# The seam between a graph attention stage and a relational attention stage: work of the second stage placed into the last steps of the first, and three reorderings in the first stage's step

## The chip, the cores and the metric

The kernel runs on one core of one Trainium2 chip. The metric is the device time of one execution in microseconds, lower is better. All tensors are in the chip's memory when it starts, and the output has to be back there when it ends.

## The reference, cut to what matters

There are 16 graphs with 512 nodes of 128 features. Three pieces of work follow one another: a graph layer, a relational attention, and a feed-forward network. All values are float32.

```python
def _gat(h, adj, W, a, out_features):
    Wh = jnp.matmul(h, W)
    e = Wh @ a[:out_features] + jnp.swapaxes(Wh @ a[out_features:], 1, 2)
    scores = jnp.where(adj > 0, jax.nn.leaky_relu(e, negative_slope=0.2), NEG)
    return jnp.matmul(jax.nn.softmax(scores, axis=1), Wh)
# graph layer
h = _gat(_gat(x, adj, W1, a1, F), adj, W2, a2, F)
h = _layernorm(x + h, g_ln1, b_ln1)
x = _layernorm(h + relu(h @ w_ff1 + b_ff1) @ w_ff2 + b_ff2, g_ln2, b_ln2)
# relational attention, 8 heads of 16
scores = jnp.einsum('bhid,bhjd->bhij', q, k) / np.sqrt(dh)
attn = jax.nn.softmax(scores, axis=-1)
for r in range(4):
    out = out + jnp.einsum('bhij,bhjd->bhid', attn * (adj == r)[:, None], v_r)
x = _ln(x + out @ Wo + bo, g1, beta1)
x = _ln(x + gelu(x @ W1 + b1) @ W2 + b2, g2, beta2)
```

The adjacency matrices of this input hold only 0 and 1. The kernel looks at all of them and takes a short path through the attention (path 0) if no other value is there, a general path (path 1) otherwise.

## The kernel before, in words

Each engine (PE is the matrix engine, DVE the vector engine, ACT the scalar engine, POOL the general one, SP the one that issues most DMAs) has its own program, written out by hand. Semaphores tie them together. There is no scheduler: each engine does its instructions in the order in which they are written, and where one waits, all behind it wait.

**The graph layer** (`graph_layer`) is software-pipelined over graphs. In step t, graph t begins (its x and adjacency are turned and multiplied by the weights), graph t-1 is in its first attention round (k = 0), graph t-2 in its second (k = 1) and its first layer norm, and graph t-3 is in the small feed-forward and its second layer norm. There are 19 steps, 0 to 18, for B = 16 graphs: 0 to 3 are written out, 4 to 14 are a loop, 15 to 18 are written out. Steps 16 to 18 only drain: in step 18 only the feed-forward of graph 15 is left.

In a step, DVE does this in order: scores of the second round (`leak` L666 and `mask` L673 for four chunks of rows), the array of absent edges (`no_edge` L774), scores of the first round (same lines), between them the reciprocal of the second round's sums (`invert`, L700), the sum behind the feed-forward (`y_t` L782), the reciprocal and the scaling of the first round's rows (`scale_rows` L707), statistics and shift of the second layer norm (L717, L724, L738), then sum, statistics and finish of the first layer norm (L794, L717, L724, L731). ACT copies, exponentiates (L645) and takes the inverse roots of the layer norms as a logarithm and an exponential (`rstds`, L651 and L658). `hw` (L610) is ACT's copy of the first round's product out of the bank `pair`; from it PE spreads a row (L467, `spread_row`), and the next step's second-round scores start. `centre` is L633 on ACT, and `xs` (L619) the stage's result. POOL scales `hw_n` (L812), which the second round (`round_two`, L493) waits for, and turns the next graph's adjacency into codes (`encode`, four L381). Codes are turned by PE (L443), kept as bytes in `codes`, and held for the attention.

In step 18 the first graph's queries and keys are made in the bank `pair` and split into three bf16 parts, written to a scratch tensor and read back stacked by heads (`FirstQueries`; L241 product, L221, L226, L231, L236 parts). Also there, `see` ORs all graphs' codes together (L747 to L761) so that the attention can choose its path.

**The attention** (`attention`, a new block with a barrier ahead of it) runs in turns of one graph, each of 8 steps s (2 groups of 4 heads by 4 chunks of rows). In a step PE makes four products `peak` (L1003), each of which DVE reduces to its largest value (L1251), for a place 6 steps ahead (`LEAD = 6`); two products `score` per half step (L1018), whose largest values come from those peaks; and the weighted sums (L1042). ACT exponentiates `prob` (L1116); POOL and DVE multiply by the mask (L1387, L1265). Turn -1 does only what must lie ahead of graph 0: 24 peaks, the values, the masks, queries and keys of graph 1. Before it stand the constants on POOL (L1366 to L1372) and the choice of path (L988, L1235, L1238, then a load of the flag and a branch on every engine).

**The feed-forward** (`feed_forward`) follows. It is not touched.

## Time and profile before

| what | value |
| --- | --- |
| median of 3 runs | 1249.26 us (1248.03 to 1250.36) |
| the profiled execution's own time | 1250.93 us |
| its span in the trace | 1249.1 us |
| PE busy | 1092.9 us (87%) |
| DVE busy | 962.1 us (77%) |
| ACT busy | 742.4 us (59%) |
| POOL busy | 614.3 us (49%) |

The time is read against the profiled execution: 1250.93 us, of which 1249.1 us are the span that the trace shows. Busy time counts an engine at work and not one that is waiting, and it is an average over three stages that are limited differently, so the stages are read one by one. A matrix instruction's end is modelled in the trace, so its busy time is no proof of full speed.

### The profile page before, as it was taken

How to read it: one execution, taken by the hardware profiler on the slowest of the kernel's cores; microseconds unless marked ns; L12 is line 12 of the kernel's file. 1: busy time of each engine (PE TensorE's matmuls, PEld its weight loads, DVE VectorE, ACT ScalarE, POOL GpSimd, SP SyncE). 2: the span in 40 equal slices, each digit the busy share in tenths (PEclk: the TensorE clock that was granted, in tenths of full speed). 3: DMA queues.
4: the chain of work that ended last, by engine and by line, in shares of the span. 5: the costliest groups of instructions: out<-in, count | busy, mean ns of one | idle time of the engine just before them, and what ended most of it. 6: DMA issues, size and time to landing. Idle time of an engine off the chain costs nothing. (4 is left out here: it accounts for less than half of the span.)

```text
span 1249.1 us, 21656 instructions
## 1 busy us (share of the span) xinstructions
PE 1092.9 (87%) x6087; PEld 501.8 (40%) x6087; DVE 962.1 (77%) x2313; ACT 742.4 (59%) x1341; POOL 614.3 (49%) x515
## 2 busy tenths in 40 slices
PE   4588888888888549999999999999999999979996
PEld 3465665665664312233332333323333233234443
DVE  2878878878877537788888888888888888618777
ACT  3477677677675323666666666666666666644442
POOL 3311311311300135878887788878888787900000
PEclk9799999999998857999999999999999999979998
DMA  5222112112100242321333213332133320000000
GB/s 168 92 76 77 50 63 88 50 54 97 50 1 1 86 118 70 106 66 50 111 110 97 69 53 109 110 93 70 57 109 110 89 73 8 2 0 34 34 34 34
DMA packets 49413, 86.50 MB, mean 69 GB/s; under 512 B 8787, under 2 KB 35795, under 8 KB 44246
## 3 DMA queue, kind: packets, MB, share of 16 engines
q1 hardware_dynamic: 46454, 85.56, 22.3%
q10 hardware_dynamic: 2912, 0.40, 0.2%
q8 instruction: 20, 0.33, 0.1%
q14 instruction: 27, 0.22, 0.1%
HBM read 52.12 MB, written 29.36 MB: 65 GB/s over the span
## 5 line engine op out<-in xcount | busy, mean ns | idle before, releaser
L1387 POOL TENSOR_TENSOR b_picked<-b_prob,b_mask 128x512 f32<-128x512 f32 x384 | 473.4, 1260 | 129.8 <-ACT b_prob L1116 129.7
L1251 DVE TENSOR_REDUCE b_top<-b_peak 128x1 f32<-128x512 f32 x512 | 343.6, 687 | 87.7 <-PE b_peak L1003 82.6
L1116 ACT ACTIVATE b_prob<-b_score 128x1024 f32<-128x1024 f32 x256 | 262.0, 1023 | 193.3 <-PE b_score L1018 191.5
L812 POOL TENSOR_TENSOR a_hw_n<-a_hw,a_inv 128x512 f32<-128x512 f32 x16 | 19.5, 1219 | 274.2 <-DVE a_inv L700 261.1
L1042 PE MATMUL b_o_ps<-b_picked,b_dval 128*32 128x512 f32 x1024 | 136.4, 604 | 12.7 <-DVE b_picked L1265 10.2
L1042 PE MATMUL b_o_ps<-b_prob,b_val 128*32 128x512 f32 x1024 | 136.3, 604 | 0.3 <-ACT b_o_t L1127 0.3
L1265 DVE TENSOR_TENSOR b_picked<-b_prob,b_mask 128x512 f32<-128x512 f32 x128 | 113.0, 883 | 1.5 <-ACT b_prob L1116 1.4
L1003 PE MATMUL b_peak<-shared 96*128 96x512 bf16 x256 | 103.4, 409 | 3.6 <-DVE b_top L1251 3.5
L645 ACT ACTIVATE a_att<-a_att,a_least 128x512 f32<-128x512 f32 x128 | 91.1, 716 | 17.3 <-DVE a_least L673 16.8
L1003 PE MATMUL b_peak<-b_k_stack,b_q_stack 96*128 96x512 bf16 x256 | 98.3, 384 | 0.0
L673 DVE CUSTOM_DVE_ANT_0 a_att<-a_att,a_no_edge 128x512 f32<-128x512 f32 x128 | 97.2, 778 | 0.0
L381 POOL TENSOR_SCALAR a_code<-a_adj_in 128x512 bf16<-128x512 int32 x64 | 73.3, 1146 | 38.6 <-DMA a_adj_in<-in_adj 23.7
L493 PE MATMUL a_turn<-a_hw_n,a_att 128*128 128x128 f32 x512 | 63.4, 284 | 25.3 <-POOL a_hw_n L812 25.3
L1504 ACT ACTIVATE c_hid<-c_mid,bff 128x512 f32<-128x512 f32 x64 | 44.0, 688 | 62.6 <-PE c_mid L1482 62.6
L1018 PE MATMUL b_score<-shared 98*128 98x512 bf16 x256 | 77.3, 383 | 0.0
L1018 PE MATMUL b_score<-b_q_stack,b_k_stack 98*128 98x512 bf16 x256 | 76.5, 379 | 0.0
L493 PEld LDWEIGHTS a_turn<-a_hw_n,a_att 128*128 128x128 f32 x512 | 60.8, 198 | 37.4 <-issue 37.4
L479 PE MATMUL a_mid<-a_h_t,wff 128*128 128x512 f32 x128 | 65.1, 636 | 11.1 <-ACT a_h_t L569 11.1
L485 PE MATMUL a_out<-a_hid,wff 128*128 128x512 f32 x128 | 59.2, 605 | 17.8 <-ACT a_hid L639 17.8
L1003 PEld LDWEIGHTS b_peak<-shared 96*128 96x128 bf16 x256 | 25.2, 98 | 113.9 <-DVE b_top L1251 98.8
L651 ACT ACTIVATE a_lnv<-a_mv,eps 128x4 f32<-128x4 f32 x32 | 9.5, 298 | 102.1 <-DVE a_mv L724 102.1
L1003 PEld LDWEIGHTS b_peak<-b_k_stack,b_q_stack 96*128 96x128 bf16 x256 | 24.6, 96 | 108.8 <-DVE b_top L1251 93.8
(176 smaller groups left out, 1807.6 us busy)
## 6 DMA issues: line engine op xcount, KB each, us to landing
a_adj_in<-in_adj SPq DMA_DIRECT2D x16, 1024.0 KB, 5.4
scratch<-shared SPq DMA_DIRECT2D x32, 384.0 KB, 2.6
shared<-scratch SPq DMA_DIRECT2D x16, 768.0 KB, 6.8
scratch<-shared SPq DMA_DIRECT2D x32, 256.0 KB, 2.6
b_q_stack<-scratch SPq DMA_DIRECT2D x8, 768.0 KB, 5.5
b_k_stack<-scratch SPq DMA_DIRECT2D x8, 768.0 KB, 8.0
a_x_in<-in_x SPq DMA_DIRECT2D x16, 256.0 KB, 2.7
xs<-in_x SPq DMA_DIRECT2D x16, 256.0 KB, 5.5
```

Source lines behind the costliest of these rows:

```text
L381: eng.tensor_scalar(code[:, c, :].rearrange("p (k q) -> p k q", k=C), adj_in[:, c, :].rearrange("p (q k) -> p k q", k=C), CODE_HI, CODE_LO ...
L479: pe.matmul(mid[f % 2][:, :], w["wff1"][0][:, f * P:(f + 1) * P], h_t[:, :], start=True, stop=True).then_inc(mid_done, 1)
L493: mm = pe.matmul(turn[:, ic * D:(ic + 1) * D], att[1][:, jc, ic * P:(ic + 1) * P], hw_n[:, jc, :], start=(jc == 0), stop=(jc == C - 1))
L645: act.activation(att[k][:, c, :], att[k][:, c, :], ACT.Exp, bias=least[k][:, c:c + 1], scale=-1.0, accum_out=total[k][:, c:c + 1]).then_in ...
L673: dve.tensor_tensor_reduce(att[k][:, c, :], att[k][:, c, :], no_edge[:, c, :], 1.0, HIGHEST, ALU.add, ALU.min, least[k][:, c:c + 1]).then_ ...
L1003: pe.matmul(peak[hh % 2][:, :], q_stack[par][0:K, h, c * P:(c + 1) * P], k_stack[par][0:K, h, :], start=True, stop=True).then_inc(sem("pea ...
L1018: mm = pe.matmul(score[u][:, k, :], k_stack[par][:, h, c * P:(c + 1) * P], q_stack[par][:, h, :], start=True, stop=True)
L1042: mm = pe.matmul(o_ps[32 * hh:32 * hh + 32, :], v[:, c, GH * g + hh, :], src[:, hh, :], start=(c == 0 and rel is None), stop=(c == C - 1 a ...
L1116: act.activation(prob[s % 2][:, 2 * u:2 * u + 2, :], score[u][:, :, :], ACT.Exp, scale=float(DH) ** -0.5).then_inc(sem("exp_ready"), 1)
L1251: dve.tensor_reduce(top[g][:, hh, c:c + 1], peak[hh % 2][:, :], AX.X, ALU.max, negate=True).then_inc(sem("peak_read"), 1)
L1265: dve.tensor_tensor(picked[(NR * s + rel) % 2][:, hh, :], prob[s % 2][:, hh, :], m, ALU.mult).then_inc(sem("picked_dve"), 1)
L1387: pool.tensor_tensor(picked[(NR * s + rel) % 2][:, hh, :], prob[s % 2][:, hh, :], m, ALU.mult).then_inc(sem("picked_pool"), 1)
```

## The change

What it does, piece by piece:

- **Steps 16 to 18 become a tail written by hand** in each engine's program. Into it go the attention's turn -1: queries and keys of graph 0 and graph 1 and their stores to scratch, graph 0's values, its mask, its 24 peaks with the reductions, and the turning, splitting and loading of the first group's largest values. The attention then starts at turn 0. The 24 products go through three PSUM banks in turn (before: two).
- **The OR of the codes** is one instruction of 512 words per step, behind `scale_rows`; only the last three instructions (`judge`) and the choice of the flag stay in the tail.
- **POOL's `encode`** waits for that OR (`codes_seen`) and no longer for the last mask of the first round (`masked[0]`).
- **The copy `hw`** stands ahead of the first layer norm's inverse root on ACT.
- **The reciprocal of the second round's sums** stands ahead of the fourth `leak` and not behind it.
- **The constants**: the two rows of ones under each key stack come by DMA from an array of ones (before: two memsets on POOL, L1366); graph 0's share of the others is set in step 3.

```diff
@@ FirstQueries
+    def peak(self, pe, banks, n):
+        R6, g, s, hh = 6 * self.z.DH, n // 16, n // 4, n % 4
+        h, c = 4 * g + hh, s % 4
+        if n == 0:
+            pe.wait_ge(self.sem("stacked"), 32)
+        if n >= len(banks):
+            pe.wait_ge(self.sem("peak_read"), n - len(banks) + 1)
+        pe.matmul(banks[n % len(banks)], self.q_stack0[0:R6, h, c * P:(c + 1) * P], self.k_stack0[0:R6, h, :],
+                  start=True, stop=True).then_inc(self.sem("peak_ready"), 1)
...
@@ steps
-            for t in range(B - 1, B + 3):
-                step(t, t < B, t - 1 < B, t - 2 < B, True, False)
+            step(B - 1, True, True, True, True, False)
...
@@ tensor
+            def tail():
+
+                spread_row(1, B - 2)
+                turn_h(B - 3)
...
+                first_qk.product(pe, pair[:, 0, :], 0, 0)
+                first_qk.product(pe, pair[:, 1, :], 0, 1)
+                for f in range(FC):
+                    feed_up(B - 3, f)
+                feed_down(B - 3)
...
+                turn_h(B - 1)
+                peaks(3, 5)
+                turn_n(B - 2)
+                for f in range(FC):
+                    feed_up(B - 1, f)
+                    peaks(5 + 2 * f, 7 + 2 * f)
+                feed_down(B - 1, (13, 15, 16, 16, 16))
+                pe.wait_ge(sem_b("values0_kept"), 2)
+                first_qk.turn_top(pe, row[0])
+                peaks(16, 18)
+                turn_y(B - 1)
+                peaks(18, 20)
+                pe.wait_ge(other_made, 1)
+                pe.transpose(pair[0:1, 1, 0:P], other[:, :], ident[:, :]).then_inc(other_turned, 1)
+                turn_n(B - 1)
+                peaks(20, 24)
@@ scalar
                 if feed:
                     rstds(1, t - 3)
                     centre(t - 3)
+                if first:
+                    keep_hw(t - 1)
                 if second:
                     rstds(0, t - 2)
-                if first:
-                    act.wait_ge(hw_done, t)
...
@@ vector
                 for c in chunks:
                     if c + 1 < C:
+                        if c == 2:
+                            between()
                         leak(k, b, c + 1, s2)
-                    if c == 2 and k == 0:
-                        between()
                     mask(k, b, c)
...
+            def see(b):
+                words = codes[:, b, :, :].rearrange("p c n -> p (c n)").bitcast(I32)
+                first = isinstance(b, int) and b == 0
+                if not first:
+                    dve.wait_ge(codes_seen, b)
+                dve.tensor_tensor(seen[:, :], words if first else seen[:, :], words, ALU.bitwise_or).then_inc(codes_seen, 1)
...
                     invert(0, t - 1)
                     scale_rows(t - 1)
+                    see(t - 1)
...
+                most(0, 16)
+                first_qk.split_top(dve, row[0])
+                add_h(B - 1)
+                most(16, 18)
+                norm_stats(1, B - 1)
+                most(18, 20)
+                norm_shift(B - 1)
...
+                most(20, 24)
@@ gpsimd
                 if more:
                     if first:
-                        pool.wait_ge(masked[0], C * t)
+                        pool.wait_ge(codes_seen, t)
                     encode(pool, t + 1, range(C))
...
@@ attention
-            for b in range(-1, 2):
-                turn(b, b % 2)
+            for b in range(2):
+                turn(b, b)
```

On DVE, inside a loop step of the graph layer, from the third `mask` of the first round to the statistics of the second layer norm, before:

```order
L666 SCALAR_TENSOR_TENSOR a_att<-a_row,a_s_own,a_low 128x512
L700 RECIPROCAL a_inv<-a_total 128x4
L671 REGISTER_ALU
L673 ISA a_att,a_least<-a_att,a_no_edge 128x512
```

and at the same place in the change, with what now stands behind the row scaling:

```order
L897 RECIPROCAL a_inv<-a_total 128x4
L863 SCALAR_TENSOR_TENSOR a_att<-a_row,a_s_own,a_low 128x512
L868 REGISTER_ALU
L870 ISA a_att,a_least<-a_att,a_no_edge 128x512
...
L904 TENSOR_SCALAR a_xw_n<-shared,a_inv 128x130
L943 TENSOR_TENSOR a_seen<-a_seen,codes 128x512
L914 BN_STATS a_stats<-a_mid 128x6 x4
```

The reciprocal has changed places with the fourth `leak`, and one instruction `seen` of 128x512 has come in ahead of the statistics.

On ACT, at the end of a loop step, from the centring of graph t-3 (`a_y`) to the result `xs`, before:

```order
L633 ACTIVATE a_y<-a_mid,a_shift,a_rstd 128x128 x4
L651 ACTIVATE a_lnv<-a_mv,eps 128x4
L658 ACTIVATE a_rstd<-a_lnv 128x4
L610 COPY a_hw<-a_pair 128x520
L614 REGISTER_ALU
L615 ISA
```

and in the change:

```order
L829 ACTIVATE a_y<-a_mid,a_shift,a_rstd 128x128 x4
L809 COPY a_hw<-a_pair 128x520
L847 ACTIVATE a_lnv<-a_mv,eps 128x4
L854 ACTIVATE a_rstd<-a_lnv 128x4
L738 REGISTER_ALU
L739 ISA
```

The copy `a_hw` has moved ahead of the logarithm and the exponential.

On PE, the seam of the two stages from the last transposes of the graph layer to the attention's first scores, before (L988 reads the flag, L1054 are queries and keys of graph 1, L1003 peaks, L1018 scores):

```order
L988 MATMUL b_misc<-ident,other 1x128
L942 TENSOR_LOAD b_general
L942 ISA x2
L943 COMPARE_AND_BRANCH
L1054 MATMUL b_misc<-xs,wq 128x512
L1054 MATMUL b_misc<-xs,wk 128x512
L1003 MATMUL b_peak<-shared 128x512 x17
L1069 MATMUL b_misc<-ident,b_top 16x128
L1003 MATMUL b_peak<-shared 128x512 x8
L1018 MATMUL b_score<-shared 128x512 x2
```

and in the change (L305 are the peaks in the tail, L567 and L573 the feed-forward of graph 15, L1245 a peak and L1260 the scores of turn 0):

```order
L305 MATMUL a_pair<-shared 128x512
L567 MATMUL a_mid<-a_h_t,wff_0 128x512
L305 MATMUL a_row<-shared 128x512
L305 MATMUL a_turn<-shared 128x512
...
L1186 TENSOR_LOAD general
L1186 ISA x2
L1187 COMPARE_AND_BRANCH
L1245 MATMUL b_peak<-shared 128x512
L1260 MATMUL b_score<-shared 128x512 x2
```

24 peaks now stand among the feed-forward and the transposes of graph 15, and behind the branch one peak and the first scores follow at once.

## Rows read from the trace of the kernel before

**Rows 1.** Windows (length, busy of PE, PEld, DVE, ACT, POOL, clock, DMA): four stretches.

```profile
326.15:349.65 23.50, 19.38 (x129) 14.31 (x128) 19.42 (x54) 16.71 (x39) 5.80 (x5) 1.00 0.19 67
...
418.75:447.20 28.45, 13.47 (x32) 6.09 (x32) 14.67 (x20) 8.71 (x16) 3.64 (x3) 0.68 0.38 111
447.20:480.19 32.99, 22.80 (x44) 6.61 (x45) 17.64 (x30) 6.04 (x14) 12.18 (x12) 0.50 0.39 114
480.19:1095.00 614.81, 602.38 (x3581) 187.00 (x3579) 511.51 (x919) 398.39 (x611) 503.44 (x412) 1.00 0.27 78
```

**Rows 2.** Timeline of a loop step: start and length in us, engine, instruction, [idle before].

```profile
336.70 0.75 DVE L666 SCALAR_TENSOR_TENSOR a_att<-a_row,a_s_own,a_low 128x512 f32<-128x512 f32 x1
...
337.79 1.22 POOL L812 TENSOR_TENSOR a_hw_n<-a_hw,a_inv 128x512 f32<-128x512 f32 x1 [16.73 <-DVE a_inv L700]
338.03 1.52 DVE L673 CUSTOM_DVE_ANT_0 a_att<-a_att,a_no_edge 128x512 f32<-128x512 f32 x1
...
339.15 3.81 PE L493 MATMUL a_turn<-a_hw_n,a_att 128*128 128x128 f32 x32 [1.10 <-POOL a_hw_n L812]
...
339.88 4.82 POOL L381 TENSOR_SCALAR a_code<-a_adj_in 128x512 bf16<-128x512 int32 x4 [0.87 <-DVE a_least L673]
...
340.77 1.75 DVE L707 TENSOR_SCALAR a_xw_n<-shared,a_inv 128x130 f32 x4 [0.15 <-DVE a_inv L700]
...
343.44 0.89 DVE L717 BATCH_NORM_STATS2 a_stats<-a_mid 128x6 f32<-128x128 f32 x4 [0.91 <-PE a_mid L425]
...
345.46 0.16 DVE L738 SCALAR_TENSOR_TENSOR a_shift<-a_mv,a_rstd 128x4 f32<-128x4 f32 x1 [0.60 <-ACT a_rstd L658]
345.66 1.50 ACT L633 ACTIVATE a_y<-a_mid,a_shift,a_rstd 128x128 f32<-128x128 f32 x4 [0.23 <-DVE a_shift L738]
...
347.89 0.30 ACT L651 ACTIVATE a_lnv<-a_mv,eps 128x4 f32<-128x4 f32 x1 [0.73 <-DVE a_mv L724]
...
348.33 0.57 ACT L610 COPY a_hw<-a_pair 128x520 f32<-128x520 f32 x1
348.57 1.12 DVE L731 TENSOR_SCALAR a_y<-a_y,a_mv,a_rstd 128x128 f32<-128x128 f32 x4 [0.72 <-ACT a_rstd L658]
348.81 0.20 ACT L615 COPY a_s_own<-shared 128x4 f32 x1
...
350.33 1.41 DVE L666 SCALAR_TENSOR_TENSOR a_att<-a_row,a_hw,a_low 128x512 f32<-128x512 f32 x2 [0.65 <-issue]
```

**Rows 3.** Timeline: the row scaling of step 15, in which POOL encodes nothing.

```profile
363.92 0.88 DVE L707 TENSOR_SCALAR a_xw_n<-shared,a_inv 128x130 f32<-128x130 f32 x4
```

**Rows 4.** Tile view: the shift of 128x4 in the attention and in the graph layer.

```profile
L1337 DVE SCALAR_TENSOR_TENSOR b_shift<-b_mv,b_rstd x16: 161/519/1116, 550.1 to 1107.6; 128x4 f32<-128x4 f32 x16
L738 DVE SCALAR_TENSOR_TENSOR a_shift<-a_mv,a_rstd x16: 161/164/165, 85.6 to 443.2; 128x4 f32<-128x4 f32 x16
```

**Rows 5.** Timeline of the seam, from step 18 to the attention's first score.

```profile
425.35 1.02 PE L241 MATMUL a_pair<-xs,wk 128*128 128x512 f32 x2
...
426.29 3.70 PE L485 MATMUL a_out<-a_hid,wff 128*128 128x512 f32 x8
...
427.87 2.28 DVE L747 TENSOR_TENSOR a_att<-codes 128x2048 int32<-128x2048 int32 x1
...
436.93 0.69 DVE L755 TENSOR_TENSOR a_att<-a_att 128x512 int32<-128x512 int32 x1
...
439.18 0.74 DVE L782 SCALAR_TENSOR_TENSOR a_y_t<-a_out,columns,a_h_t 128x512 f32<-128x512 f32 x1
...
446.15 0.78 ACT L619 ACTIVATE xs<-a_mid,columns 128x512 f32<-128x512 f32 x1 [1.21 <-PE a_mid L431]
...
452.58 2.08 PE L1054 MATMUL b_misc<-xs,wq 128*128 128x512 f32 x2 [4.97 <-issue]
...
464.38 9.05 DVE L1251 TENSOR_REDUCE b_top<-b_peak 128x1 f32<-128x512 f32 x13 [1.87 <-PE b_peak L1003]
```

**Rows 6.** Line view of the peaks: min, median, max ns at PE.

```profile
L1003 PE MATMUL b_peak<-shared x256: 377/382/634, 458.1 to 1031.3; 96*128 96x512 bf16 x128
```

More of the change, by code:

```diff
@@ new lines, in move @@
+    def move(self, sp):
+        R6 = 6 * self.z.DH
+        sp.dma_start(self.x_own[:, :], self.xs[:, 0, :, :].rearrange("p c d -> p (c d)")).then_inc(self.sem("x_own"), 16)
+        load_ones(sp, self.w, self.k_stack0).then_inc(self.sem("ones_in0"), 16)
+        for b in range(2):
+            for n in range(2):
+                for t in range(3):
+                    sp.wait_ge(self.sem(f"part{t}_ready{n}"), b + 1)
+                    store_part(sp, self.scratch[b], self.parts[n], n, t).then_inc(self.sem(f"parts_out{n}"), 16)
+            if b == 0:
+                for n in range(2):
+                    sp.wait_ge(self.sem(f"parts_out{n}"), 48)
+                    sp.dma_start((self.q_stack0, self.k_stack0)[n][0:R6, :, :],
+                                 stack_rows(self.scratch[0, n])).then_inc(self.sem("stacked"), 16)
@@ new lines, in values, with keep_values @@
+    def values(self, pe, bank, half):
+        D, w = self.z.D, self.w
+        for k in range(2):
+            c = 2 * half + k
+            at = bank[:, 2 * k * D:2 * (k + 1) * D]
+            pe.matmul(at, w["ones"][:, :], w["bias3"][:, 0:2 * D], start=True, stop=False)
+            mm = pe.matmul(at, self.x_own[:, c * P:(c + 1) * P], w["wv"][:, 0:2, :].rearrange("p r d -> p (r d)"),
+                           start=False, stop=True)
+        mm.then_inc(self.sem("values0_done"), 1)
+    def keep_values(self, act, bank, half):
+        D, DH = self.z.D, self.z.DH
+        act.wait_ge(self.sem("values0_done"), half + 1)
+        for k in range(2):
+            c = 2 * half + k
+            src = bank[:, 2 * k * D:2 * (k + 1) * D].rearrange("p (r h d) -> p r h d", r=2, h=HEADS)
+            act.copy(self.val0[:, c, :, 0:DH], src[:, 0, :, :])
+            last = act.copy(self.dval0[:, c, :, 0:DH], src[:, 1, :, :])
+        last.then_inc(self.sem("values0_kept"), 1)
@@ new lines, in mask @@
+    def mask(self, act, half):
+        chunks = slice(2 * half, 2 * half + 2)
+        act.copy(self.mask0[:, chunks, :], self.codes[:, 0, chunks, :])
+    def peak(self, pe, banks, n):
[7 more added lines that the diff above has]
+                  start=True, stop=True).then_inc(self.sem("peak_ready"), 1)
@@ L258, with load_ones @@
+def load_ones(eng, w, stack):
+    rows = stack[6 * 16:6 * 16 + 2, :, :].rearrange("r h n -> r (h n)")
+    return eng.dma_start(rows.rearrange("r (a q) -> r a q", q=P), w["ones"][0:2, :].unsqueeze(1).to_broadcast([2, HEADS * 4, P]))
 BLOCKS = 6
@@ L909, in count @@
             def count(turn, end):
-                return sum(0 <= t + by < end for t in range(-2, turn + 1)
+                return sum(0 <= t + by < end for t in range(turn + 1)
                            for n, (_, _, _, by) in enumerate(ITEMS[path]) if t < turn or n < pos)
```

421 lines of the change are left out of this document (273 added, 148 removed).

## The prediction

> **What bounds the kernel now.** I read the windows by stage first, then the timeline of one loop step, then the timeline of the seam. The attention runs 614.81 us with PE busy for 602.38 of them at a granted clock of 1.00 [rows 1]: it is PE's, the change leaves its turns 0 to 15 as they are, and they move as a block. The change works on two other places.
>
> The first is the loop step of the graph layer, 23.50 us long, in which neither PE (19.38 busy) nor DVE (19.42) is full [rows 1]. A chain through four engines sets it. DVE's scores end in the reciprocal of the second round; POOL scales `hw_n` at 337.79 (it had idled 16.73 us for that reciprocal); PE's second round starts at 339.15, 1.10 us idle for POOL; behind it PE turns the feed-forward's result, for which DVE's statistics wait 0.91 us until 343.44. They give the shift at 345.46 and ACT's centring until 345.66 + 1.50 = 347.16. Then ACT does logarithm, exponential, the copy `hw` at 348.33, and two more, and only then the lowered row, for which DVE's next `leak` waits until 350.33 [rows 2].
>
> The second is the seam. Step 18 takes 28.45 us and turn -1 another 32.99 [rows 1], 61.44 us together, with every engine half idle. In step 18 the OR of the codes holds DVE from 427.87 to 439.18, and `y_t`, which PE waits for, stands behind it; the stage ends with `xs` at 446.15 + 0.78 = 446.93, PE's first product comes at 452.58, and from 464.38 the reductions of the peaks run back to back, 9.05 / 13 = 0.70 us each [rows 5].
>
> **The change part by part.**
>
> *Copy ahead of the root.* Between the centring's end (347.16) and the logarithm (347.89) ACT has 0.73 us in which it waits for DVE; the copy takes 0.57 and fits. What followed the copy moves up by 348.81 - 348.33 = 0.48 us. DVE can take it: its layer norm ends at 348.57 + 1.12 = 349.69, 0.64 ahead of the `leak` [rows 2]. Gain 0.48 per step.
>
> *Reciprocal ahead of the fourth leak.* It comes earlier by that instruction, 0.75 us (336.70), and with it POOL, PE's second round and the statistics [rows 2]. The mask behind it stalls on POOL's scaling either way (1.52 us at 338.03 [rows 2]), once, so DVE's scores end as before. Gain 0.75, if the statistics find DVE free.
>
> *The OR in the step.* 0.69 us for 128x512 [rows 5], fifteen times on DVE. What hides it is the 0.91 us wait for PE [rows 2], and that shrinks by the 0.75 above. But POOL's encoding (339.88, 4.82 us) now starts behind the OR, and so no longer runs beside the row scaling, which took 1.75 us with it and 0.88 without [rows 2, 3]. So scaling ends at 340.77 + 0.88 = 341.65, the OR at 342.4, and the statistics could start at 343.44 - 0.75 = 342.69. It fits by 0.3 us; without that cover it would cost up to 0.69 a step.
>
> *Encoding later.* It runs from about 342.7 to 347.4. PE needs the codes behind the next step's transposes, from about 349: 1.6 us to spare. What it newly meets is the shift of 128x4, which would now be issued at 345.46 - 0.75 = 344.7, in the midst of the encoding. It reads two arrays in SBUF. In the graph layer before, with POOL idle, it never took over 0.165 us; in the attention, with POOL busy, 0.161 / 0.519 / 1.116 [rows 4]. So it costs between 0 and 0.95 us, and the centring and DVE's whole rest of the step stand behind it. I take the median, 0.519 - 0.161 = 0.36: both engines' rhythm is fixed here, so the true value is one number within the bounds, and I can't place it better.
>
> This is where a rule of the Trainium skill speaks against the change. "SBUF — State Buffer", section "Who interferes with whom", says that a vector instruction with two SBUF inputs contends with a GpSimd instruction that reads SBUF, and that the one that comes second blocks for the whole instruction of the other. By that rule the shift waits for the rest of an encoding instruction, the OR would too if it ran beside one (it doesn't, POOL waits for it), and the statistics, with one input, don't. The trace agrees, with the spread from 0.161 to 1.116.
>
> *Sum of the steps.* 0.48 + 0.75 - 0.36 = 0.87 us in steps 3 to 14 (twelve): 10.4. Step 15 has no encoding, 1.2. Against that the first OR stands ahead of DVE's preparation in step 1 (0.69), and in step 2 the copy ahead of the root waits for a slow first round: I take 1.2 together. **A = -10.4 us**; bounds from 12 x 0.28 - 1 = 2 to 12 x 1.23 + 1 = 16.
>
> *Steps 16 and 17.* They take on, for two graphs, four products of 1.02 us on PE [rows 5], four first and four second parts on ACT, four remainders on DVE like a `leak` (0.75 [rows 2]), four third parts on POOL that meet DVE's masks as above, and three short instructions that judge the OR. In step 16 DVE has no slack: remainders 1.5, one or two collisions 1, and some of ACT's parts ahead of `hidden`. In step 17 DVE had long waits and takes its share there. Against it stand the 0.48 of the copy twice and the 0.75 of the reciprocal. **B = +1 us**, between -1 and +4.
>
> *The seam.* Now 61.44 us. Then, counted on DVE from the end of step 17: 24 reductions x 0.70 = 16.7 [rows 5]; splitting, `y_t`, statistics, shift and flag 3.3. PE holds it up in the middle: a feed-forward product (3.70 / 4 = 0.93 [rows 5]) and two peaks (2 x 0.38 [rows 6]) against 1.40 of DVE, 0.3 to 0.5 four times, and the last product's 3.70 with three peaks, 4.8 against 2.1: 4.3 in all. The last four peaks stand behind the transposes of the centred array: 1.50 for the centring, 0.9 around it. Sum 26.7. Then the barrier, load of the flag and branch: from 446.93 to 452.58 it was 5.65, with the flag's making in it, which is now done earlier; I take 4.8 (4 to 5.65), and 0.7 for a peak and the scores. 32.2 in all. The parts, stacks and rows of ones are on SP's queue some 20 us before the peaks need them, and graph 1's stack, issued behind the branch, has two attention steps. **C = 32.2 - 61.4 = -29.2 us**, between -25 and -32.
>
> **Sum:** -10.4 + 1 - 29.2 = -38.6. The profiled execution took 1250.93, so 1212.3; it stands 1.67 above the median of the runs, 1249.26, so I forecast a median of **1211**.
>
> **The rivals.**
>
> 1. *The collision eats the loop's gain.* Each shift (or the OR, if statistics come sooner than I count) pays the full price: 0.95, leaving 0.28 per step and A at 2 to 3 us. For it: the row scaling paid 1.75 - 0.88 = 0.87 beside POOL [rows 2, 3]. Against: the median. 1219.
> 2. *The tail runs at the lower clock.* In step 18 the granted clock averaged 0.68, in turn -1 it was 0.50, the level of 1.2 GHz [rows 1]. At that level PE's share of the tail (24 peaks 9.1, feed-forward 7.4, transposes 2.5) doubles from 19 to 38 us, against 26.7 counted: +11, 1222. Against: the tail keeps PE busy where before it sat still for the OR.
> 3. *Slower.* The attention enters behind 5 us without PE work and stays at the lower clock. Each microsecond there loses half, PE being busy 602.38 of 614.81 [rows 1]; from 77 us on at that level the change loses, 1251. Against: before, it came out of 33 us at 0.50 and the attention's mean was still 1.00. The Trainium skill ("TensorE: Matmul & The Clock Gate", Part 1) says that the throttled state is the default and that activity releases it, which would speak for an early rise too.
> 4. *The change doesn't do what it says:* the prologue's chain (parts, scratch, stack, largest values) isn't ready when the tail wants it, and engines wait there. Half of C's overlap lost, 1226.
> 5. *Better:* the shift falls into a gap between two encodings and the branch costs 4: 1203.
>
> **How the numbers follow.** My forecast (1205 to 1216) 0.52, rival 1 0.20, rival 2 0.12, rival 3 0.03, rival 4 0.03, rival 5 0.10. From 1203 to 1223 the range takes in the forecast, rivals 1 and 2 and the edge of rival 5. No change means within 0.2%, about 2.5 us, which is what a measurement of this kernel can tell. All cases but rival 3 are faster: 0.96, 0.01, 0.03.
>
> **What would show it.** The distance of two lowered rows in the loop: 22.6 us (23.2 by rival 1). The row scaling at 0.88, the shift between 0.16 and 1.1, the statistics' wait gone to near zero. From the last layer-norm finish of graph 15 to the end of the stage about 27 us, the first `score` near 441, and 610 us of attention behind it. Wrong would be: a clock of 0.50 over the tail, a wait of PE for `stacked`, encodings that end after PE wants them, or an attention longer than 616.

## The result, and the profile after

| | before | after |
| --- | --- | --- |
| median | 1249.02 us (1248.03 to 1250.36, 4 runs) | 1198.62 us (1197.11 to 1200.78, 4 runs) |
| ratio | | 0.9597 (0.958 to 0.9615) |
| span of the profiled execution | 1249.1 us | 1196.6 us |

The changed kernel is 50.4 us faster by the medians (52.5 by the two spans). The forecast was 1211, the range 1203 to 1223: the sign was right, the gain was too small by 12 us, and the range missed the time by 4.4 us.

The windows of the changed kernel, with the columns of [rows 1]: a loop step; the tail's second part from its first lowered row to the last layer-norm finish; from there to the attention's first score; the attention.

```profile
312.73:335.11 22.38, 19.62 (x128) 14.38 (x128) 18.97 (x56) 16.79 (x40) 5.52 (x5) 1.00 0.20 71
379.56:399.06 19.50, 15.75 (x73) 9.11 (x71) 14.16 (x46) 9.99 (x23) 3.27 (x3) 1.00 0.32 100
399.06:428.97 29.91, 18.17 (x57) 8.07 (x57) 17.84 (x40) 11.68 (x27) 1.96 (x5) 0.75 0.05 12
430.06:1041.09 611.03, 600.04 (x3560) 186.14 (x3560) 509.23 (x914) 396.56 (x608) 499.91 (x409) 1.00 0.29 81
```

The stretches of before that answer to the second and third are these:

```profile
396.01:418.69 22.68, 15.11 (x60) 8.54 (x60) 10.58 (x37) 10.11 (x23) 1.04 (x1) 0.85 0.01 1
418.69:480.19 61.50, 36.27 (x76) 12.71 (x77) 32.31 (x51) 14.75 (x30) 15.82 (x14) 0.58 0.39 112
```

So the seam became 61.50 - 29.91 = 31.6 us shorter and the step ahead of it 22.68 - 19.50 = 3.2. The attention moved as a block: from first to last `b_prob` 610.1 us before (481.3 to 1091.4), 611.0 after (430.1 to 1041.1). All before the seam is read off ACT's first lowered row of each step:

| first `a_low` of step | 4 | 6 | 14 | 16 | 17 |
| --- | --- | --- | --- | --- | --- |
| before, us | 89.73 | 137.04 | 326.15 | 372.82 | 396.01 |
| after, us | 88.83 | 133.82 | 312.73 | 356.83 | 379.56 |

By step 16 the change has gained 372.82 - 356.83 = 16.0 us; step 16 itself gives 0.5 more. From step 6 to 14 a step is (326.15 - 137.04) / 8 = 23.64 us before and (312.73 - 133.82) / 8 = 22.36 after: 1.28 each, where the forecast had 0.87.

The timeline of that loop step, to be laid beside [rows 2]:

```profile
312.73 0.59 ACT L822 ACTIVATE a_low<-a_row 128x512 f32<-128x512 f32 x1
...
323.83 1.04 POOL L1064 TENSOR_TENSOR a_hw_n<-a_hw,a_inv 128x512 f32<-128x512 f32 x1 [12.37 <-DVE a_inv L897]
...
328.14 0.69 DVE L943 TENSOR_TENSOR a_seen<-a_seen,codes 128x512 int32<-128x512 int32 x1
...
329.14 4.72 POOL L467 TENSOR_SCALAR a_code<-a_adj_in 128x512 bf16<-128x512 int32 x4 [4.26 <-DVE a_seen L943]
...
329.30 0.89 DVE L914 BATCH_NORM_STATS2 a_stats<-a_mid 128x6 f32<-128x128 f32 x4 [0.48 <-PE a_mid L513]
...
331.32 0.16 DVE L935 SCALAR_TENSOR_TENSOR a_shift<-a_mv,a_rstd 128x4 f32<-128x4 f32 x1 [0.60 <-ACT a_rstd L854]
331.52 1.51 ACT L829 ACTIVATE a_y<-a_mid,a_shift,a_rstd 128x128 f32<-128x128 f32 x4 [0.23 <-DVE a_shift L935]
...
332.91 0.60 ACT L809 COPY a_hw<-a_pair 128x520 f32<-128x520 f32 x1
```

The OR is hidden: behind it the statistics still wait 0.48 us for PE. The shift is issued while POOL encodes (329.14 to 333.86) and yet takes 0.16 us, in all eleven full loop steps. That is the collision term of the sum, and it wasn't paid. The seam, in the order of time:

```profile
397.98 1.08 DVE L928 TENSOR_SCALAR a_y<-a_y,a_mv,a_rstd 128x128 f32<-128x128 f32 x4
...
399.05 0.68 DVE L311 TENSOR_REDUCE top<-a_pair 128x1 f32<-128x512 f32 x1
...
404.01 0.69 DVE L311 TENSOR_REDUCE top<-a_turn 128x1 f32<-128x512 f32 x1 [1.88 <-PE a_turn L305]
404.62 0.68 DVE L311 TENSOR_REDUCE top<-a_pair 128x1 f32<-128x512 f32 x1
...
412.92 0.28 DVE L321 CAST top_hi<-a_row 16x128 bf16<-16x128 f32 x1 [1.14 <-PE a_row L316]
...
418.25 0.14 DVE L1020 TENSOR_SCALAR general<-a_widest 1x1 int32<-1x1 f32 x1
421.20 0.69 DVE L311 TENSOR_REDUCE top<-a_turn 128x1 f32<-128x512 f32 x1 [2.81 <-PE a_turn L305]
...
423.00 0.68 DVE L311 TENSOR_REDUCE top<-a_turn 128x1 f32<-128x512 f32 x1
```

```profile
419.62 1.11 PE L519 MATMUL a_mid<-ident,a_y 128*128 128x128 f32 x4 [4.19 <-ACT a_y L829]
...
428.57 0.61 PE L1245 MATMUL b_peak<-shared 96*128 96x512 bf16 x1 [6.01 <-issue]
428.97 1.06 PE L1260 MATMUL b_score<-shared 98*128 98x512 bf16 x2
```

The stage ends with DVE's last reduction at 423.68, PE's first product comes 4.9 us later, and DVE had sat 2.81 us ahead of the last four reductions, for peaks that stand on PE behind the transposes of the last centred array.

### The profile page after: what moved, and what is told of

It is laid out like the page before. It is cut to its first block and busy times, and to the rows that moved or that the text cites. A ratio compares the mean times of both kernels' runs of the same rounds, so it can differ in the third digit from the quotient of the medians.

```text
span 1196.6 us, 21640 instructions
## 1 busy us (share of the span) xinstructions
PE 1076.5 (90%) x6087; PEld 496.7 (42%) x6087; DVE 948.1 (79%) x2324; ACT 741.5 (62%) x1341; POOL 602.8 (50%) x513
## 5 line engine op out<-in xcount | busy, mean ns | idle before, releaser
L1489 DVE TENSOR_REDUCE top<-b_peak 128x1 f32<-128x512 f32 x488 | 327.8, 687 | 89.4 <-PE b_peak L1245 85.2
L1622 POOL TENSOR_TENSOR b_picked<-b_prob,mask 128x512 f32<-128x512 f32 x192 | 236.2, 1257 | 61.7 <-ACT b_prob L1360 61.6
L1622 POOL TENSOR_TENSOR b_picked<-b_prob,b_mask 128x512 f32<-128x512 f32 x192 | 237.3, 1263 | 53.6 <-ACT b_prob L1360 53.6
L1064 POOL TENSOR_TENSOR a_hw_n<-a_hw,a_inv 128x512 f32<-128x512 f32 x16 | 16.7, 1041 | 211.8 <-DVE a_inv L897 198.9
L1245 PE MATMUL b_peak<-b_k_stack,b_q_stack 96*128 96x512 bf16 x256 | 98.3, 384 | 0.0
L1245 PE MATMUL b_peak<-shared 96*128 96x512 bf16 x232 | 89.9, 389 | 6.0 <-issue 6.0
L1260 PE MATMUL b_score<-shared 98*128 98x512 bf16 x256 | 77.6, 384 | 0.0
L1260 PE MATMUL b_score<-b_q_stack,b_k_stack 98*128 98x512 bf16 x256 | 76.5, 380 | 0.0
L573 PE MATMUL a_out<-a_hid,wff 128*128 128x512 f32 x128 | 59.5, 605 | 18.5 <-ACT a_hid L835 18.5
L1286 PE MATMUL b_o_ps<-b_picked,b_dval 128*32 128x512 f32 x512 | 68.2, 604 | 7.7 <-DVE b_picked L1503 5.2
L1286 PE MATMUL b_o_ps<-b_picked,dval 128*32 128x512 f32 x512 | 68.2, 604 | 5.0 <-DVE b_picked L1503 5.0
L1245 PEld LDWEIGHTS b_peak<-b_k_stack,b_q_stack 96*128 96x128 bf16 x256 | 24.6, 96 | 108.7 <-DVE top L1489 93.8
L1286 PE MATMUL b_o_ps<-b_prob,b_val 128*32 128x512 f32 x512 | 68.2, 604 | 0.3 <-ACT b_o_t L1371 0.3
L1286 PE MATMUL b_o_ps<-b_prob,val 128*32 128x512 f32 x512 | 68.2, 605 | 0.0
L593 PE MATMUL a_pair<-a_xw_n,a_att 128*128 128x130 f32 x512 | 62.4, 281 | 4.8 <-DVE a_xw_n L904 4.8
```

Source lines behind the costliest of these rows:

```text
L593: mm = pe.matmul(pair[:, ic // 2, at:at + D + 2], att[0][:, jc, ic * P:(ic + 1) * P], xw_n[:, jc, :], start=(jc == 0), stop=(jc == C - 1))
L1245: pe.matmul(peak[hh % 2][:, :], q_stack[par][0:K, h, c * P:(c + 1) * P], k_stack[par][0:K, h, :], start=True, stop=True).then_inc(sem("pea ...
L1260: mm = pe.matmul(score[u][:, k, :], k_stack[par][:, h, c * P:(c + 1) * P], q_stack[par][:, h, :], start=True, stop=True)
L1286: mm = pe.matmul(o_ps[32 * hh:32 * hh + 32, :], v[:, c, GH * g + hh, :], src[:, hh, :], start=(c == 0 and rel is None), stop=(c == C - 1 a ...
L1489: dve.tensor_reduce(top[g][:, hh, c:c + 1], peak[hh % 2][:, :], AX.X, ALU.max, negate=True).then_inc(sem("peak_read"), 1)
L1622: pool.tensor_tensor(picked[(NR * s + rel) % 2][:, hh, :], prob[s % 2][:, hh, :], m, ALU.mult).then_inc(sem("picked_pool"), 1)
```

## The experiments

Each lists the median and its ratio to the kernel before with the 95% interval. "Step" is the distance of the first lowered rows from step 6 to step 14, divided by 8. It tells more than the total: executions with the same code in steps 0 to 3 reached step 4 between 86.96 us (the kernel with the old norm order) and 88.83 us (the changed kernel), so two totals can differ by about 2 us before the loop begins. A second spread lies behind the attention, where no run changed anything: from the last `b_prob` to the feed-forward's first product (`c_mid`) it is 16.7 to 16.9 us in nine of the fourteen profiles, at a mean granted clock of 0.91 to 0.95, and 18.2 to 19.0 us in five (the kernel before, the reciprocal alone, the codes alone, the loop's three edits, the step without the OR), at 0.67 to 0.73.

### The three edits of the loop, one by one and together

**Copy alone**, on the kernel before:

```diff
+                if first:
+                    ... act.copy(hw ...).then_inc(hw_ready, 1)
                 if second:
                     rstds(0, t - 2)
-                if first:
-                    ... act.copy(hw ...).then_inc(hw_ready, 1)
```

> The kernel before, with one edit: in each step ACT's copy hw stands ahead of the first layer norm's inverse root. Recorded theory: the copy fits into the 0.73 us in which ACT waits for DVE's statistics, so what follows moves up by 0.48 us; 13 steps with both (3 to 15) and two more in the drain make -6 to -7 us, 1242 to 1243 us, a loop step of 23.16 instead of 23.64 us. Rival: the root now comes later by what is left of the copy, DVE's layer-norm finish with it, and DVE's next leak then waits for nothing else; the gain would be 0 to 0.2 us a step, 1246 to 1249 us.

Measured: 1242.26 us, 0.9947 (0.9931 to 0.9964); step 23.09, -0.55. The theory held, a little better than its 0.48.

**Reciprocal alone**, on the kernel before:

```diff
                     if c + 1 < C:
+                        if c == 2:
+                            between()
                         leak(k, b, c + 1, s2)
-                    if c == 2 and k == 0:
-                        between()
```

> The kernel before, with one edit: the reciprocal of the second round's sums stands ahead of the fourth leak. POOL still encodes behind the last mask, beside the row scaling. Recorded theory: the chain through POOL, PE's second round and DVE's statistics moves up by 0.75 us, in the 12 or 13 full steps: -9 to -10 us, 1239 to 1240 us, a loop step of 22.9 us. Rival 1: the shift, issued 0.75 us earlier, now falls into the last encoding instruction (which ends at 344.70 us in the step read) and pays up to 0.95 us: no gain. Rival 2: the row scaling at 1.75 us beside the encoding ends at 342.5 us and holds the statistics, so 0.5 us a step and not 0.75: 1242 us.

Measured: 1242.2 us, 0.9936 (0.9919 to 0.9952); step 23.41, only -0.23. Rival 2 named the right place; that its total (1242) came true is partly luck, since it had 0.5 us a step, and this execution was 2.3 us ahead by step 4 (87.44 for 89.73). Timeline of the loop step, DVE and POOL:

```profile
311.67 4.72 POOL L381 TENSOR_SCALAR a_code<-a_adj_in 128x512 bf16<-128x512 int32 x4 [1.48 <-DVE a_least L673]
...
312.67 2.64 DVE L707 TENSOR_SCALAR a_xw_n<-shared,a_inv 128x130 f32 x4 [0.15 <-DVE a_inv L700]
...
315.23 0.88 DVE L717 BATCH_NORM_STATS2 a_stats<-a_mid 128x6 f32<-128x128 f32 x4
```

PE has the statistics' input ready sooner, but the row scaling now takes 2.64 us beside the encoding (1.75 in [rows 2], 0.88 with POOL idle [rows 3]), and the statistics follow it without a wait. Most of the 0.75 us stays there. Where POOL encodes nothing the reciprocal gives it all: steps 15 and 16 take 22.30 us each, for 23.17 and 23.19 before.

**OR and encoding alone**, on the kernel before (step 18 keeps only the three instructions that judge the OR):

```diff
                     scale_rows(t - 1)
+                    see(t - 1)
...
-                        pool.wait_ge(masked[0], C * t)
+                        pool.wait_ge(codes_seen, t)
```

> The kernel before, with one edit: the OR of the codes as one instruction of 512 words a step behind the row scaling, POOL's encoding behind it; in step 18 only the three short instructions that judge it. Copy and reciprocal stand where they stood. Step 18 loses 11.3 us of OR on DVE and gets back 2.0: -9.3 us where y_t waited for it, -4 to -9 if PE's chain is next. In the loop, recorded theory: the OR is hidden (scaling ends 0.87 us sooner), the shift collides with the encoding at 0.36 us a step on average, +4 us: 1243 to 1245 us. Rival: the shift meets no instruction in its way and takes 0.16 us, as in the changed kernel: loop step unchanged at 23.64 us, 1240 us.

Measured: 1246.33 us, 0.9971 (0.9961 to 0.9981); step 24.01, **+0.37**. Here the shift does collide, in all ten steps of the window from 100 to 350 us (tile view of that window: least, median, greatest ns):

```profile
L738 DVE SCALAR_TENSOR_TENSOR a_shift<-a_mv,a_rstd x10: 605/619/629, 111.5 to 327.6; 128x4 f32<-128x4 f32 x10
```

In the step read, an encoding instruction begins at 327.05 (the row below covers it and the next, 1.11 us of work each) and so ends near 328.16. The shift, issued at 327.56, ends at 328.18:

```profile
327.05 2.31 POOL L381 TENSOR_SCALAR a_code<-a_adj_in 128x512 bf16<-128x512 int32 x2
```

That the step's +0.37 is so near the 0.36 of the theory is luck: the shift is 0.46 longer, of which some 0.2 is won back behind it (see below), and it is issued 0.11 later behind the lowered row (19.42 us for 19.31).

By step 16 this kernel is 6.35 us behind (379.17 against 372.82), 2.0 of them before step 4 already. From the last layer-norm finish (424.60) to the first score (476.12) it then takes 51.5 us where the kernel before took 61.50: the OR's removal from step 18 is worth 10.0 us.

**All three, with the old steps 16 to 18 and turn -1:**

```diff
+ the three diffs above together
```

> The kernel before with all three edits of the step (copy, reciprocal, OR with encoding behind it), but with steps 16 to 18 and turn -1 as they were. It measures term A with the same steps as the recorded sum, apart from the tail. Recorded theory: 0.87 us a step, A = -10.4 us, and step 18 without the OR: -9.3 us; together 1229 us. By the trace of the changed kernel (22.37 us a step, -16.0 us by step 16): 1223 us. If the three edits hinder or help one another, the sum of the three single ones (taken over the loop step) differs from this one's.

Measured: 1224.07 us, 0.9788 (0.977 to 0.9806); step 22.36, exactly the changed kernel's; at step 16 356.92 us, 15.9 ahead. The expectation from the trace held (1223), the recorded sum didn't (1229). The three single effects add to -0.55 - 0.23 + 0.37 = -0.41 us a step, the three together give -1.28. The 0.87 between them is two collisions that each edit has alone and not in company: the row scaling's with the old place of the encoding, and the shift's with its new place. By the single runs they cost 0.75 - 0.23 = 0.52 and 0.37, 0.89 together.

**The encoding back behind the mask**, on the changed kernel:

```diff
-                        pool.wait_ge(codes_seen, t)
+                        pool.wait_ge(masked[0], C * t)
```

> The changed kernel with one edit: POOL's encoding waits for the last mask of the first round again, as before the change; copy, reciprocal and OR stay. Theory: the encoding then lies beside the row scaling, which takes 2.64 us as in the kernel with the reciprocal alone (0.88 now), and the OR behind it waits too; the statistics come 1.2 to 2 us later than now: a loop step of 23.4 us or more, +12 us: 1208 to 1216 us. So the encoding's move is what lets the reciprocal's 0.75 us through. Rival: copy and reciprocal give their 0.48 + 0.23 us by themselves and the OR is hidden: 22.95 us a step, 1205 us.

Measured: 1210.78 us, 0.9694 (0.9678 to 0.971); step 23.56, +1.20. The theory's time held. Timeline:

```profile
337.35 5.21 POOL L467 TENSOR_SCALAR a_code<-a_adj_in 128x512 bf16<-128x512 int32 x4 [1.48 <-DVE a_least L870]
...
338.34 2.64 DVE L904 TENSOR_SCALAR a_xw_n<-shared,a_inv 128x130 f32 x4 [0.15 <-DVE a_inv L897]
...
340.91 0.68 DVE L943 TENSOR_TENSOR a_seen<-a_seen,codes 128x512 int32<-128x512 int32 x1
341.51 0.88 DVE L914 BATCH_NORM_STATS2 a_stats<-a_mid 128x6 f32<-128x128 f32 x4
```

Copy, reciprocal and OR without the encoding's move are worth 23.64 - 23.56 = 0.08 us a step. The scaling is at 2.64 us again, the OR follows it and the statistics follow the OR, none of them with a wait: the OR is no longer hidden. So the 1.20 that the move is worth are the 0.75 - 0.23 = 0.52 of the reciprocal and the 0.68 of the OR. The copy doesn't need it: alone, with the encoding in its old place, it gave its 0.55.

### Is the shift's 0.16 us luck of the phase?

In the changed kernel an encoding instruction runs from 330.32 to 331.43 and the next begins at 331.51 (tile rows of one instruction each, below). The shift, issued at 331.32, ends at 331.48, in the gap.

```profile
330.32 1.11 POOL L467 TENSOR_SCALAR a_code<-a_adj_in 128x512 bf16<-128x512 int32 x1
331.51 1.14 POOL L467 TENSOR_SCALAR a_code<-a_adj_in 128x512 bf16<-128x512 int32 x1
```

**OR left out of the step, encoding earlier:**

```diff
-                    see(t - 1)
...
-                        pool.wait_ge(codes_seen, t)
+                        pool.wait_ge(scaled[0], t)
```

> The changed kernel with less work: the OR of the codes is left out of every step (the look then sees graph 15's codes only, which changes no path for this input), and POOL's encoding starts behind the row scaling itself, about 0.65 us sooner. Theory of the phase: a shift issued while an encoding instruction runs ends when that instruction ends. Instructions of 1.18 us that began at 329.14 us end at 330.32 and 331.50, so the shift issued at 331.32 pays nothing; beginning at 328.5 they end at 330.86 and 332.04, and the shift pays 0.5 to 0.56 us. So with less work the kernel is slower by 12 x 0.5 = 6 us: 1204 to 1206 us, shift at 0.65 to 0.75 us, a loop step of 22.9 us. Rival: a small operand of 128x4 waits only by chance, the shift stays near 0.16 us and the time at 1198 to 1199 us; or the OR was on the path, and the time falls below 1195 us.

**Encoding later by one small instruction:**

```diff
+            if not isinstance(b, int):
+                eng.tensor_scalar(idle[:, :], adj_in[:, 0, 0:128], CODE_HI, CODE_LO, ALU.min, ALU.max)
             for c in chunks:
```

> The changed kernel with one more instruction of POOL ahead of each encoding in the loop (128 columns into an array that nobody reads, some 0.35 us). Nothing waits for it but the encoding. Theory of the phase: the border between two encoding instructions moves from 331.50 to about 331.85 us, the shift issued at 331.32 waits for it: 0.5 us instead of 0.16, +0.35 us a step in 11 steps, +3.5 to +4 us: 1202 to 1203 us. Rival: the price is a fixed one for any meeting; the shift stays at 0.16 us and the time at 1198 to 1199 us.

The shift in the same window, without the OR and then with the delay:

```profile
L935 DVE SCALAR_TENSOR_TENSOR a_shift<-a_mv,a_rstd x11: 697/729/745, 107.0 to 333.0; 128x4 f32<-128x4 f32 x11
```

```profile
L938 DVE SCALAR_TENSOR_TENSOR a_shift<-a_mv,a_rstd x11: 467/479/507, 106.3 to 331.1; 128x4 f32<-128x4 f32 x11
```

Its length was foretold for both (0.65 to 0.75 us, and 0.5), and is neither a chance nor a fixed price. The times moved less than foretold: without the OR 1200.32 us, 0.9597 (0.9581 to 0.9613), step 22.60, +0.23 and not 0.5; with the delay 1197.87 us, 0.9584 (0.9568 to 0.96), step 22.48, +0.12 and not 0.35. The totals can't be told from the changed kernel's (without the OR the stretch behind the attention was 18.2 us for 16.8, 1.4 of its 1.7 more); the steps can. The reason is what follows the shift. From its end to the statistics of the first norm (with the sum `add_x` between) it is 0.85 us in the changed kernel (331.48 to 332.33), but 0.64 without the OR (333.73 to 334.37), 0.63 with the delay (331.58 to 332.21) and 0.63 in the kernel with the codes' edit alone (328.18 to 328.81): behind a blocked shift the next instruction starts 0.2 us closer. So without the OR the shift is 0.57 longer, 0.22 of it comes back, and the statistics are 0.12 sooner: 0.23. With the delay 0.32 - 0.22 = 0.10. Even so, a step with less work is longer, because the encoding starts 0.72 us sooner in it (15.69 us behind the lowered row for 16.41). A kernel without the OR whose encoding keeps its place was not run.

### The tail

**Old order of the norms in its second part** (ACT's roots and centring follow it):

```diff
                 judge()
+                norm_stats(1, B - 2)
+                norm_shift(B - 2)
                 add_x(B - 1)
                 norm_stats(0, B - 1)
-                norm_stats(1, B - 2)
                 norm_finish(B - 1)
-                norm_shift(B - 2)
```

> The changed kernel with one edit in the tail's second part (graph 15 in its second round): statistics and shift of the second layer norm of graph 14 stand ahead of the sum and the first layer norm of graph 15 again, and ACT's roots and centring in that order, as in step 17 of the kernel before. Theory: this order, not the parts, made steps 16 and 17 shorter where the sum had +1 us: the first layer norm of graph 15 ends 2 us later and all of the seam with it: 1200 to 1201 us. Rival: DVE and PE do the same work in another order, and the reductions of the peaks wait for no norm: 1198 to 1199 us.

Measured: 1200.5 us, 0.9604 (0.9588 to 0.962). From the second part's first lowered row (377.76) to the end of the last norm finish (398.24 + 1.12 = 399.36) it is 21.60 us, against 19.50: the 2.1 us that the theory had. DVE's reciprocal comes 9.07 us behind the lowered row in both, so the difference lies behind it. The window of that stretch, to be laid beside 379.56:399.06:

```profile
377.76:399.36 21.60, 15.91 (x73) 9.05 (x71) 14.51 (x46) 11.48 (x27) 3.27 (x3) 0.97 0.29 90
```

The total moved by 1.9, within what two executions differ by; the stretch is what shows it.

**Two banks for the 24 peaks, not three:**

```diff
-        peak_banks = [pair[:, 0, :], row[1][:, :], turn[:, :]]
+        peak_banks = [pair[:, 0, :], row[1][:, :]]
...
-                peaks(0, 3)
+                peaks(0, 2)
...
-                peaks(3, 5)
+                peaks(2, 5)
```

> The changed kernel with the 24 first peaks going through two PSUM banks in turn, as in turn -1 of the kernel before (three in the changed one). Theory 1: the third bank is why the reductions follow one another at 0.60 to 0.69 us and not at the 0.70 us of the recorded sum; with two they go at 0.70, +1.4 us: 1200 us. Theory 2: the pace is DVE's own and the 0.70 us belonged to the lower clock of turn -1; then 1198 to 1199 us, and the reductions at 0.64 us where PE is at the full clock.

Measured: 1199.0 us, 0.9599 (0.9583 to 0.9615). By the total theory 2 held, and at the full clock most reductions follow one another at 0.60 to 0.69 us with two banks too. The stretch shows a part of theory 1 as well. Where a peak takes PE 0.61 us instead of 0.38, one reduction follows the other after 0.79 (398.62 to 399.41) and 0.78 us (420.72 to 421.50), where three banks have 0.59 and 0.60, and once DVE waits 0.27 us for a peak. From the last norm finish to the end of the last reduction it is 25.35 us (397.44 to 422.79) against 24.6: the third bank is worth 0.7 us, half of what theory 1 had.

**Last four peaks ahead of the last transposes:**

```diff
+                peaks(20, 24)
                 turn_n(B - 1)
-                peaks(20, 24)
```

> The changed kernel with one edit in the tail: the last four peaks stand ahead of the transposes of the last centred array on PE, not behind. In the changed kernel DVE had done everything at 418.39 us and waited 2.81 us for them until 421.20. Theory: the four reductions then run during the centring, and the stage ends with xs at 421.55 us instead of with the last reduction at 423.68: -2.1 us, 1196 to 1197 us. Rival: the peaks run into PE's transposes or the barrier waits for something else (the row of ones on SP's queue, POOL's start of the block at 423.96 us): 1198 to 1199 us.

Measured: 1194.79 us, 0.9563 (0.9547 to 0.9578). The theory held. DVE's last four reductions run from 418.12 on, while ACT centres; from the last norm finish to the first score:

```profile
398.70:426.59 27.89, 18.47 (x56) 8.03 (x57) 17.75 (x40) 11.67 (x27) 1.95 (x5) 0.78 0.05 11
```

That is 27.89 us against 29.91. The total is 3.8 us lower; 2.0 of it are this edit's. In the kernel with both edits below, the same stretch is 28.60 us (397.74 to 426.34), 0.4 of the difference on the way from the last instruction to PE's first product.

**xs behind the lowered row, and both together:**

```diff
                 if second:
                     lower(1, t - 2)
+                if feed and not (isinstance(t, int) and t == 3):
+                    keep_x(t - 4)
...
-                if feed:
-                    keep_x(t - 3)
```

> The changed kernel with one edit in the step: ACT's write of xs stands behind the next step's first lowered row. In the step read, low stands ready on PE 0.4 us before ACT comes to it, and DVE's leak waits 0.57 us for it behind its own layer-norm finish. Theory: DVE's finish is next, 0.57 us a step are gained in 12 steps: -6 to -7 us, 1192 us, a loop step of 21.8 us. Rival: ACT's later work (turned x, second lowered row, h_t) is 0.6 us later against DVE and PE, the feed-forward's sum or the first round waits for it: gain of 0.2 us a step or none, 1196 to 1199 us.

> The changed kernel with two edits together: the last four peaks ahead of the last transposes, and xs written behind the next step's first lowered row. If they add: -2.1 and -1.9 us, 1194 to 1195 us. If the second was only a difference between executions: 1196 to 1197 us.

Measured: 1196.69 us, 0.9568 (0.9552 to 0.9584), and both edits 1194.32 us, 0.9559 (0.9543 to 0.9575). The step is 22.30 in both, -0.07: the rival held. DVE no longer waits for the lowered row (its finish ends at 311.40, its `leak` begins at 311.61), and 10 us later waits for ACT's exponential, which it didn't before:

```profile
321.53 0.18 DVE L897 RECIPROCAL a_inv<-a_total 128x4 f32<-128x4 f32 x1 [0.19 <-ACT a_att L841]
```

ACT's write of `xs` only changed whom it holds up. The two candidates together can't be told from the peaks' edit alone (1194.79). Both of these are below every time of the changed kernel, whose lowest is 1197.11.

## Why the prediction was right or wrong

By its own three terms:

| term | forecast, us | measured, us |
| --- | --- | --- |
| A, steps to 15 | -10.4 (2 to 16 gained) | -16.0 |
| B, steps 16 and 17 | +1 (-1 to +4) | -3.6 |
| C, the seam | -29.2 (-25 to -32) | -31.6 |
| attention and behind | 0 | -1.3 |

The last is the rest to the -52.5 of the spans: the attention +0.9, its end to the feed-forward's start 16.8 us for 18.7, what is left is under half a microsecond. The 1.9 are luck: the mean granted clock there was 0.94 after and 0.67 before, and the kernel with the copy alone, whose attention and tail are the old ones, had 16.8 us at 0.95 too.

**Copy ahead of the root:** right, 0.55 for 0.48.

**Reciprocal ahead of the fourth leak:** right in company (the shift comes 331.32 - 312.73 = 18.59 us behind the lowered row, 345.46 - 326.15 = 19.31 before: 0.72 for 0.75). The text gave as its condition that scaling and OR end before the statistics could start, by 0.3 us. They did, by 0.48. Alone, without the encoding's move, it gave 0.23.

**The OR in the step:** right, hidden, and only with the encoding's move; with the old place it costs its 0.68.

**Encoding later** is a failed step. The sum took 0.36 us for the shift's collision, the median of another stage's spread, with the words that the true value is one number within the bounds. It was 0, the bottom of the bounds. The text had what the phase is made of: an encoding from 342.7 us in instructions of 1.2, a shift at 344.7, so a border at 345.1 and a wait of 0.4. The real shift was issued 2.18 us behind the encoding's start and the border came at 2.29, 0.1 us later, so that the shift was not delayed at all. An error of 0.3 us in a start decides here, so the phase could not be forecast, but its two ends should have stood as two cases, and the price was too high for another reason: 0.2 us of any wait is got back behind the shift. In all rows read here the second to come waits until the first one's instruction ends, whichever its own size, and so its wait depends on when it comes. The rule of the Trainium skill ("SBUF — State Buffer", section "Who interferes with whom") says the same, that the one that comes first holds the shared path for its whole instruction and the other blocks. Of the 5.6 us that A missed, 4.1 lie in the steps 4 to 14, 0.37 a step: this term's 0.36 and the copy's 0.07 cover them. Step 15 gave 0.25 more than forecast. The last 1.2 lie before step 4, where executions of the same code differ by up to 1.9, so they are not shown to be the change's.

**Steps 16 and 17 (B)** is the step that failed most for its size, -3.6 where the range was -1 to +4. It counted the work that was put in and not the order in which the tail was written. The kernel with the loop's edits and the old tail tells the two apart: its step 16 takes 21.63 us and its step 17, to the end of the last norm finish (401.52), 22.97, against 22.73 and 19.50 in the changed kernel. So the added work costs 1.1 us in step 16, and the rewritten step 17 is 3.5 shorter in spite of it. The tail does the first norm of the last graph ahead of the second norm of the one before it, and that alone gives 2.1 us (the kernel with the old order). Another 1.2 lie ahead of DVE's reciprocal, which comes 9.07 us behind the lowered row for 10.30 before. There the feed-forward's product of graph 14 is shorter, before and after:

```profile
397.63 5.40 PE L479 MATMUL a_mid<-a_h_t,wff 128*128 128x512 f32 x8 [0.87 <-ACT a_h_t L569]
```

```profile
381.93 3.89 PE L567 MATMUL a_mid<-a_h_t,wff 128*128 128x512 f32 x8 [0.87 <-ACT a_h_t L802]
```

The granted clock was 0.66 from 398 to 403 us before and 1.00 over the second part after; in the kernel with the loop's edits and the old tail the product was still 5.40, with a clock of 0.66 from 380 to 385 us. The tail puts products for queries and keys ahead of it. That they keep the clock up is argued from these rows, and no run isolated it.

**The seam (C)** was right in mechanism and a little too dear. From the last norm finish (399.06) to the end of the last reduction (423.68) it is 24.6 us for 26.7:

| part | forecast | measured |
| --- | --- | --- |
| 24 reductions | 16.7 | 15.1 |
| short work on DVE | 3.3 | 3.1 |
| PE holds it up in the middle | 4.3 | 1.88 + 0.62 + 1.14 = 3.6 |
| the last centring | 2.4 | 2.8 |

A reduction comes every 0.63 us and not every 0.70: the row of [rows 5] was read in a stretch at half the clock and with two banks. The end with branch, peak and score took 5.3 for 5.5. The OR that left the seam was worth 10.0 us of the term.

**The rivals.** Rival 1 (collision eats the gain) is found in the kernel with the codes' edit alone, though the shift pays 0.46 there and not 0.95. Rival 2 (low clock in the tail): the second part ran at 1.00, and in the third it fell to 0.75 on average, but DVE and the centring set the end there, and the seam was 2.4 us shorter than forecast and not 11 longer. Rival 3 (attention at half clock) did not occur: 611.0 us with a mean clock of 1.00, the granted clock 0.55 from 430 to 435 us and 1.00 in the windows behind. The Trainium skill ("TensorE: Matmul & The Clock Gate", Part 1) says that activity releases the throttle, and the trace agrees: PE was busy for all of the 5.00 us at 0.55, and 1.00 followed. Rival 4 did not occur: no peak waited for a stack. Rival 5 was nearest: the shift did fall into a gap, though the branch cost 4.9 and not 4. Its price was added up wrongly: 12 x 0.36 = 4.3 for the gap and 0.8 for the branch make 1206, which lies inside the forecast's own band, and not 1203. So no case in the working gives the lower end of the range. The time fell below it by the rewritten step 17, the shorter seam and 1.9 us of luck, which no rival had.

## What to carry to other kernels

DVE and POOL held each other up here for the rest of the running instruction. Where two such engines have a fixed rhythm, ask at which place of the other's instruction an operation comes: the answer is one number, and any edit upstream changes it, one that removes work too. Reorderings around such a meeting don't add: test them together before dropping one that lost alone.

When a stretch is rewritten, price the new order and not only the work that is put in: who comes first of two independent chains was worth 2.1 us here, and the added instructions cost 1.1 in step 16.

When DVE idles near the end of a stage for a product that itself waits for nothing, the product stands behind a waiting instruction on PE's queue: swapping the two gave 2 us.

## What the runs showed of the hardware

- The shift of 128x4 took 0.16, 0.48, 0.62 or 0.73 us, depending only on where it met an encoding instruction of 1.11 us on POOL, and ended in the steps read within 0.05 us of that instruction's end or in the gap of 0.08 us between two.
- The row scaling, four instructions with a single array and a column of scalars as inputs, meets the same block: 0.88, 1.75 or 2.64 us, 0.87 and 0.89 more each time. POOL's series of four took 4.72 us beside a scaling of 2.64 (the kernel with the reciprocal alone), no more than beside none.
- The block works the other way too. Where the OR began at 340.91 and POOL's fourth encoding at 340.98 (the kernel with the encoding back behind the mask), the OR took its usual 0.68 us and the encoding 1.58 instead of 1.11. This makes the series 5.21 us there.
- DVE's next instruction starts about 0.2 us closer behind a shift that was blocked than behind a free one (0.63 or 0.64 us instead of 0.85 to the instruction after it).
- POOL's scaling of `hw_n` took 1.04 us where it began beside a `leak` of DVE (which reads its row from PSUM), and 1.22 us where it began beside a `mask`.
- From the last instruction of one block to PE's first product in the next, with barrier, flag and branch between and all data ready, it took 4.9 us in the changed kernel (423.68 to 428.57), 4.8 with the peaks first (421.35 to 426.19), 5.1 with two banks (422.79 to 427.88) and 5.3 with both candidates (420.68 to 425.94).
